# A planner's stage durations, travel times and turn shifts replaced in an attention and expert kernel

## What is computed

```python
x = x + tanh(g_xattn[0]) * L0_xattn(ctx, layernorm(x), b, lengths)      # unit 0: keys and values from the context
x = x + tanh(g_ffn[0])   * L0_ffn(layernorm(x), ...)                    # unit 1: self attention + 8 experts, top 2
x = x + tanh(g_xattn[1]) * L1_xattn(layernorm(x), ctx, ...)             # unit 2: context and own keys, then a projection
x = x + tanh(g_ffn[1])   * L1_ffn(layernorm(x), ...)                    # unit 3: causal attention, projection, layernorm, 8 experts, top 2
```

## Time and profile before

| | |
|---|---|
| time, median of 3 runs | 2508.11 us (2504.15 to 2510.68) |
| profiled execution, span from first to last instruction | 2498.3 us |
| what lies around the span, against the median | 9.8 us |
| PE, DVE, ACT, POOL busy share of the span | 86%, 64%, 56%, 53% |
| mean granted TensorE clock | 0.954 of 2.4 GHz |

### The profile page before, as it was taken

How to read it: one execution, slowest core, us unless ns; L and a number is a source line. 1 busy time by engine, 2 the same in 40 slices (tenths; PEclk the granted TensorE clock), 3 DMA queues, 4 the chain that set the end, 5 groups by cost and what they waited for, 6 DMA issues and landing times. The chain is left out here.

```text
span 2498.3 us, 53077 instructions
## 1 busy us (share of the span) xinstructions
PE 2158.4 (86%) x17514; PEld 1546.5 (62%) x17515; DVE 1595.7 (64%) x4064; ACT 1396.8 (56%) x2463; POOL 1315.6 (53%) x2193
## 2 busy tenths in 40 slices
PE   1898887899999999998899999999854999999990
PEld 1454454555556655565556666766633999999990
DVE  4787776843544787777767777777656444444445
ACT  3688885455556877766767777776631222222222
POOL 5555414467665553323323327888744565666553
PEclk9999999899999999999999999999976999999995
DMA  6878737335566775555556446665436422222224
GB/s 181 213 191 201 180 75 176 84 102 146 135 164 165 190 178 123 129 127 121 130 117 139 118 94 136 143 148 136 115 110 211 103 36 38 36 36 38 34 37 141
DMA packets 227041, 311.02 MB, mean 124 GB/s; under 512 B 30142, under 2 KB 163224, under 8 KB 220570
## 3 DMA queue, kind: packets, MB, share of 16 engines
q1 hardware_dynamic: 197450, 259.17, 41.8%
q0 software_dynamic: 22864, 36.66, 7.4%
q10 hardware_dynamic: 6528, 12.58, 1.4%
HBM read 206.67 MB, written 102.56 MB: 124 GB/s over the span
## 5 line engine op out<-in xcount | busy, mean ns | idle before, releaser
L1191 ACT ACTIVATE ex<-t_ps 128x512 f32<-128x512 f32 (+1 forms) x1280 | 684.3, 578 | 197.6 <-PE t_ps L1097 151.8
L1507 DVE TENSOR_REDUCE mx<-s_ps 128x2 f32<-128x512 f32 (+1 forms) x1024 | 658.7, 683 | 191.1 <-PE s_ps L1068 114.6
L1097 PE MATMUL t_ps<-qs,ks 123*128 123x256 bf16 x2048 | 363.2, 281 | 23.6 <-ACT ex L1191 12.6
L1120 PE MATMUL pv_ps<-ex,va 128*17 128x256 f32 (+1 forms) x5120 | 323.4, 380 | 0.9 <-POOL ex L1261 0.5
L1906 PEld LDWEIGHTS x_up_ps<-x_rows_t,x_wnow 128*128 128x128 f32 x2272 | 266.5, 193 | 5.3 <-issue 0.9
L1185 ACT ACTIVATE qs<-tr_ps 27x2048 bf16<-27x2048 bf16 x128 | 239.4, 1870 | 53.2 <-PE tr_ps L1081 49.9
L1906 PE MATMUL x_up_ps<-x_rows_t,x_wnow 128*128 128x128 f32 x2272 | 267.1, 276 | 1.1 <-DVE x_pre L1969 0.7
L1097 PEld LDWEIGHTS t_ps<-qs,ks 123*128 123x128 bf16 x2048 | 175.4, 100 | 147.7 <-ACT ex L1191 73.4
L1916 PE MATMUL x_y_ps<-wdn,x_act 128*128 x1136 | 257.1, 379 | 1.2 <-DVE x_y L1980 1.2
L1074 PE MATMUL s_ps<-ks,qs 99*128 99x256 bf16 (+1 forms) x1024 | 190.9, 290 | 55.5 <-DVE mx L1507 42.1
L1916 PEld LDWEIGHTS x_y_ps<-wdn,x_act 128*128 128x128 f32 x1136 | 210.3, 190 | 27.2 <-issue 1.6
(11 more groups left out here) (326 smaller groups left out, 4052.8 us busy)
## 6 DMA issues: line engine op xcount, KB each, us to landing
q_parts<-pq SPq DMA_DIRECT2D x128, 192.0 KB
qs<-q_parts SPq DMA_DIRECT2D x64, 384.0 KB, 5.0
qs<-q_parts SPq DMA_DIRECT2D x192, 128.0 KB, 5.9
k_parts<-pk SPq DMA_DIRECT2D x96, 192.0 KB
ks<-k_parts SPq DMA_DIRECT2D x96, 192.0 KB
ks<-k_parts SPq DMA_DIRECT2D x288, 64.0 KB
ks<-ctx_k_parts SPq DMA_DIRECT2D x64, 192.0 KB
ks<-ctx_k_parts SPq DMA_DIRECT2D x192, 64.0 KB
```

Source lines behind the costliest of these rows:

```text
L1097: last = pe.matmul(dst[:, t * T:(t + 1) * T], key[0:ROWS, h, t * P:(t + 1) * P], qs[q_at][0:ROWS, h, :], start=True, stop=True)
L1120: last = pe.matmul(pv_ps[i * VS:i * VS + VW, q0:T], val[:, t, k * QH + i, :], e, start=r == 0 and t == 0, stop=r == srcs - 1 and t == NT - ...
L1191: act.activation(ex[:, n % EXPS, 0:w], t_ps[n % 2][:, 0:w], ACT.Exp).then_inc(t_read, 1)
L1507: dve.tensor_reduce(dst, s_ps[n % S_BANKS][:, :].rearrange("p (a b) -> p a b", a=dst.shape[-1]), AX.X, ALU.max).then_inc(s_read, 1)
```

## The change

The stage table is rewritten. Each stage now has two figures, how long it holds its engine and how long until its result is there. Three lines of it, and what replaces `HOPS` and the single `NEAR_US`:

```diff
-    "MOE": [("dve", 1.95)],
-    "T": [("pe", 0.222), ("act", 0.6)],
-HOPS = {"pe": 0.2, "dve": 0.1, "act": 0.1, "pool": 0.15, "sp": 0.0, "wire": 0.1}
-NEAR_US = 0.05
+    "MOE": [("dve", 1.65, 1.8)],
+    "T": [("pe", 0.235, 0.42), ("act", 0.482, 0.614)],
+ARRIVE = {"pe": 0.145, "dve": 0.024, "act": 0.024, "pool": 0.07, "sp": 0.05, "wire": 0.0}
+ENGINES = ("wire", "sp", "pe", "dve", "act", "pool")
+NEAR_US = {"wire": 0.02, "sp": 0.3, "pe": 0.02, "dve": 0.1, "act": 0.06, "pool": 0.15}
```

A table shifts a step's turn, in jobs, for each unit (and for some steps each half or quarter). Two of its 48 lines, and where it acts:

```diff
+LATER = {
+    "OT": ((-33.7, -7.6), (-23.2, -7.8), (-16, -16.2), (-17.5, -25.7)),
+    "MOE": ((0,), (0,), (-5.3,), (0,)),
...
+def arrive(source, engine):
+    return 0.0 if source == engine else ARRIVE[engine]
+def part_of(step):
+    name, k = step[0], step[3]
+    return k[0] // HG if name in ("S", "T") else k if name in ("M", "MT", "ROWSK", "ROWSC") else k // (HG // QH) if name in ("PV", "OT") else 0
+def later(step):
+    return LATER[step[0]][step[1]][part_of(step)] if step[0] in LATER else 0.0
+def scored(u, b):
+    return [("T", u, b, (h, src)) for h in range(H) for src in range(sources(u))]
...
-            pick = min((x for x in found if x[0] <= soon + NEAR_US), key=lambda x: (x[1], rank(x[2]), x[0]))
+            pick = min((x for x in found if x[0] <= soon + NEAR_US[engine]), key=lambda x: (x[1] + later(x[2][0]), rank(x[2]), x[0]))
...
-        us = stages_of(s)[n][1]
-        begun[op], done[op] = now, now + us
+        _, held, took = stages_of(s)[n]
+        begun[op], done[op] = now, now + took
         if engine != "wire":
-            free[engine] = now + us
+            free[engine] = now + held
...
-            est[x] = max(est.get(x, 0.0), now + us + (0.0 if stages_of(x[0])[x[1]][0] == engine else HOPS[engine]))
+            est[x] = max(est.get(x, 0.0), now + took + arrive(engine, stages_of(x[0])[x[1]][0]))
```

Four waits are stated so that they hold in any order:

```diff
+                        if nth_x and JOBS[j - NX][0] == 0:
+                            sp.wait_ge(h_normed, HNX_AT[("HNX", *JOBS[j - NX], 0)] + 1)
...
-                            v, c = JOBS[j - NQ]
-                            sp.wait_ge(t_ready, T_AT[("T", v, c, (H - 1, sources(v) - 1))] + 1)
+                            sp.wait_ge(t_ready, max(T_AT[t] for t in scored(*JOBS[j - NQ])) + 1)
...
+                        if j >= 2:
+                            pool.wait_ge(tr_ready, TR_AT[("MT", *JOBS[j - 2], k)] + 1)
...
-                        if k == 0 and nth_o and JOBS[j - NO][0] == 3:
+                        if step == OT_FIRST[(u, b)] and nth_o and JOBS[j - NO][0] == 3:
```

More of the change, by code:

```diff
@@ new lines @@
+    "ROWSK": [("sp", 1.7, 1.7), ("wire", 5.5, 5.5)],
+    "ROWSQ": [("sp", 1.7, 1.7), ("wire", 6, 6)],
+    "ROWSC": [("sp", 1.7, 1.7), ("wire", 5.5, 5.5)],
+    "BPROJ": [("pool", 1.25, 1.29)],
+    "XB": [("pool", 1.25, 1.29)],
+    "STOREB": [("sp", 0.5, 0.5), ("wire", 7, 7)],
+    "HNS": [("dve", 0.95, 1.04)],
+    "HNP": [("pool", 1.05, 1.12)],
+    "HNX": [("dve", 0.64, 0.75)],
+    "HNG": [("pool", 2.57, 2.62)],
+    "HT": [("pe", 0.43, 0.61), ("act", 0.48, 0.61)],
+    "HG": [("pe", 0.85, 1.06), ("dve", 0.1, 0.18)],
@@ new lines @@
+    "PROJ": [("pe", 0.864, 1.03), ("pe", 0.864, 1.03), ("dve", 0.667, 0.76)],
+    "FIN": [("dve", 0.67, 0.76)],
+    "STOREX": [("sp", 0.5, 0.5), ("wire", 7.5, 7.5)],
+}
+STAGES_OF_UNIT = {
[8 rows of a table added]
+}
+ARRIVE = {"pe": 0.145, "dve": 0.024, "act": 0.024, "pool": 0.07, "sp": 0.05, "wire": 0.0}
+ENGINES = ("wire", "sp", "pe", "dve", "act", "pool")
+NEAR_US = {"wire": 0.02, "sp": 0.3, "pe": 0.02, "dve": 0.1, "act": 0.06, "pool": 0.15}
+LATER = {
+    "LOADX": ((-10,), (-3.2,), (-8.2,), (3.8,)),
+    "LOADC": ((14.2,), (0,), (-2.4,), (0,)),
+    "VC": ((-14.4,), (0,), (-2.3,), (0,)),
+    "LNS": ((-7.4,), (0,), (18.2,), (11.6,)),
+    "LNP": ((-47.8,), (0,), (-8.3,), (11.9,)),
+    "LNX": ((3.4,), (0,), (8.4,), (1.3,)),
+    "XT": ((38.8,), (14.3,), (20.1,), (25.4,)),
+    "KT": ((11.1,), (0,), (0,), (0,)),
+    "KSPLIT": ((6.1,), (12.4,), (20,), (-22.8,)),
+    "STACKK": ((-6.3,), (-17.4,), (-7.7,), (7,)),
+    "QSPLIT": ((10.3,), (11.6,), (11.2,), (0.2,)),
+    "STACKQ": ((-25,), (-35.8,), (-19.9,), (-46.5,)),
+    "ROWSK": ((-11.3, -21.9), (9.6, -7.5), (4.5, 19.5), (-40.5, -29.9)),
+    "ROWSQ": ((-5.8,), (-0.4,), (12.6,), (-5.1,)),
[6 rows of a table added]
+    "FIN": ((20.2,), (25.9,), (0,), (0,)),
+    "HNS": ((-8,), (0,), (0,), (-34.5,)),
+    "HNP": ((-23.3,), (0,), (0,), (-16.5,)),
+    "HNX": ((-37.4,), (0,), (0,), (-35.7,)),
+    "STOREN": ((-12,), (0,), (0,), (0,)),
+    "HT": ((6.4,), (0,), (0,), (27.2,)),
+    "HG": ((1.8,), (0,), (0,), (12.8,)),
+    "STOREX": ((21.2,), (13.3,), (-2.1,), (-26.5,)),
+    "LOADN": ((0,), (-25.8,), (0,), (0,)),
+    "K": ((0,), (-27.4,), (20.1,), (7.2,)),
+    "Q": ((0,), (0.8,), (10.9,), (6.3,)),
+    "V": ((0,), (-5.8,), (9.4,), (17.3,)),
+    "LOADY": ((0,), (0,), (-4.2,), (0,)),
+    "MOE": ((0,), (0,), (-5.3,), (0,)),
+    "ROWSC": ((0, 0), (0, 0), (-13.8, -13), (0, 0)),
+    "BPROJ": ((0,), (0,), (6.4,), (0,)),
+    "OTT": ((0,), (0,), (-47.1,), (-11.5,)),
+    "PROJ": ((0,), (0,), (5,), (7.4,)),
+    "XB": ((0,), (0,), (13,), (0,)),
+    "STOREB": ((0,), (0,), (4.8,), (0,)),
+    "HNG": ((0,), (0,), (0,), (-34.5,)),
+    "RC": ((0,), (1.8,), (0,), (0,)),
+    "RX": ((0,), (29.3,), (0,), (0,)),
+    "RANK": ((0,), (-8.7,), (0,), (0,)),
+    "RH": ((0,), (1.8,), (0,), (0,)),
+    "TH": ((0,), (-9.9,), (0,), (0,)),
+    "NAME": ((0,), (-15.1,), (0,), (0,)),
+    "XR": ((0,), (-29.2,), (0,), (0,)),
+    "XTT": ((0,), (-2.2,), (0,), (0,)),
+    "XE": ((0,), (-16.6,), (0,), (0,)),
+    "XS": ((0,), (34,), (0,), (0,)),
+}
@@ L121, in stages_of @@
     return STAGES_OF_UNIT.get((step[0], step[1]), STAGES.get(step[0]))
+def arrive(source, engine):
[5 more added lines that the diff above has]
+    return LATER[step[0]][step[1]][part_of(step)] if step[0] in LATER else 0.0
 def turns(step):
[L126 removed]
+    return sum(stage[0] == "pe" for stage in stages_of(step))
 def heads_of(g):
@@ L307, in can_begin @@
                     return None
-                at = done[reader] + HOPS[stages_of(reader[0])[reader[1]][0]]
+                at = done[reader] + arrive(stages_of(reader[0])[reader[1]][0], stages_of(s)[n][0])
             if name == "T" and len(had) >= EXPS:
@@ L337, in orders @@
             first += 1
-        for engine, mine in ready.items():
+        for engine in ENGINES:
             found = []
+            mine = ready.get(engine, [])
             for op in mine:
@@ L398 @@
 PV_AT = counted(of_kind("pe", "PV"))
+OT_FIRST = {s[1:3]: s for s in reversed(of_kind("dve", "OT"))}
 TR_AT = counted(of_kind("pe", "MT", "OT"))
```

58 lines of the change are left out of this document (33 added, 25 removed), and 18 rows, old and new, of tables (LATER, STAGES, STAGES_OF_UNIT).

## The result

The changed kernel took 2381.38 us (median of four, 2380.03 to 2386.21) beside 2506.13 us for the kernel before (2502.93 to 2510.68): a ratio of 0.9518, 95% interval 0.9499 to 0.9537. The profiled execution has a span of 2379.3 us against 2498.3, so 119 us are to be found in it.

What follows compares the result with a forecast made beforehand. PE's work was taken to bound attention, with idle PE and low clock to win; +2 - 12 - 20 - 22 - 6 = -58 us on a span of 2498.3, plus 9.8 added back, gave 2450 us, range 2430 to 2470.

Steps and rivals of the forecast that it cites:

- The four waits: Restated waits in the order: they name steps done long before, so they were costed at nothing.
- rival 3: Gains are half: splits still meet MOE in unit 2, the stretched choosing gives back what it fills; 2482 us, chance 0.12.
- The start: Start of the kernel: all seven token loads go ahead of the first context, +2 us, bounds 0 and +6.
- Unit 2, -22 for the pattern: Unit 2, images 9 to 15: shorter MOE and shorter PE waits save 3.1 us an image, bounds 0 and -31.
- Rest of unit 2, 0: Unit 2 outside the pattern: PE's own work, so 0; bounds +8 and -10, shared with the expert tiles.
- The choosing, -20: Choosing of experts: 72 reductions inside it instead of 30 give PE work, net -20 us, bounds 0 and -27.
- the tiles, 0: Expert tiles: PE's own work, so 0; bounds +8 and -10, shared with the rest of unit 2.
- Unit 0, -12: Unit 0: half of 18.5 us of waits and a third of the low clock won, bounds 0 and -30.
- unit 3, -6: Unit 3: half of 11.0 us of PE waits won, -6 us, bounds +3 and -12.
- Span and median: Whole kernel: 9.8 us between span and median added back to the forecast span of 2440.3 us.
- Rival 2: Order better everywhere, unit 2 beyond its fast part, unit 0 near its bound: 2392 us at the extreme, 2415 middle; chance 0.14.
- Rival 5: Nothing to measure: filled time is lost at the next place, PE's idle time being overstated; 2508 us, chance 0.07.

Runs made afterwards that it cites:

- waits_only: The kernel before, its own orders, with only the four restated waits of the change: ratio 0.9996 to the kernel before.
- before_no_adds: The kernel before with three of the four instructions adding the expert rows left out for images 9 to 15 of unit 2: ratio 0.9890.
- after_no_adds: The changed kernel with three of the four instructions adding the expert rows left out for images 9 to 15 of unit 2: ratio 0.9510.
- choosing_glued: The changed kernel with RC 9 to 13 and RC 14 to 19 of the choosing each in one piece again on DVE: 2386.28 us, ratio 0.9534.
- tile_shifts_only: The changed kernel with the turn shifts of the ten steps RC to XS alone, 0 for all steps of attention: ratio 1.0001.
- before_clear: The kernel before with the expert-row adds and layernorm statistics of images 9 to 15 four reductions earlier on DVE in unit 2: 2516.1 us, ratio 1.0049.
- [2532]: Mark of runs on chips where the kernel before, run beside, took 2530 to 2534 us.
- [2505]: Mark of runs on chips where the kernel before, run beside, took 2502 and 2504 us; the result itself is of this kind.
- before_apart: The kernel before with the layernorm statistics of images 9 to 15 of unit 2 moved two reductions behind their MOE on DVE: ratio 0.9947.

## Why the prediction was wrong

**What held.** The bound (PE, idle time and low clock), the place of every gain, the 656 us left alone, and the direction of nearly every sign named: no PE wait over 2 us in unit 2, the once-an-image line every 33.8 us (35 to 36 forecast), clock 1.00, the wait of 14.9 us gone, the first copy later. Only the last copy came earlier, not later, and unit 2 began 50 us earlier, not 30. The four waits cost nothing that shows (`waits_only`). The slowing of rival 3 is there: the adds take 1.79 us alone and 3.94 beside a split, which agrees with the lock that "SBUF — State Buffer" of the Trainium skill describes, as cited ahead. In the new order it met `MOE` in only two of the seven images, for 0.5 us each.

**The start**, +2: measured +3 by the cuts (107 instead of 104).

**Unit 2, -22 for the pattern.** Right in kind and nearly in size. By `before_no_adds` three of the four adds cost 26 us, by `after_no_adds` 2 remain, so 24 to 25 were won. The walk kept 1.3 us of waits an image and 2.5 us for `MOE`; measured are 0.3 (1.9 us in the window, six images) and 1.78.

**Rest of unit 2, 0: the step that failed.** Some 22 of the unit's 47 us came from it, as the two kernels without the adds also show (569 and 547 us); the bound that I had set was -10. The working held that what is left is "PE's own work", from one window, 1300 to 1438, at 97%. Two mistakes lie in it. First, these windows left out 205 of the unit's 595 us. They read, in the kernel before:

```profile
463.00:555.00 92.00, 84.28 (x635) 54.66 (x632) 56.09 (x122) 48.91 (x92) 58.99 (x80) 0.96 0.37 103
...
920.00:1048.00 128.00, 119.72 (x1074) 76.34 (x1072) 101.13 (x193) 93.78 (x159) 43.08 (x77) 1.00 0.54 134
1438.00:1515.00 77.00, 74.02 (x678) 49.59 (x676) 55.37 (x198) 60.94 (x104) 28.05 (x56) 1.00 0.44 101
```

The first row is of unit 1. In the other two, 8.3 + 3.0 = 11 us of idle PE stood unpriced. Second, 97% is not a bound: 34.3 us an image became 33.3 (133 us for four), at 99.4%. In the sum over the unit PE's idle time went from 41.5 to 9.6 us and its busy time from 553.5 to 538.4, which is 47. The fall in busy time is the clock's: 27 us of the unit were at half clock before, none after. To put idle PE that no large named wait accounts for at nothing failed in units 0, 1 and 3 too, but nowhere by as much.

**The choosing, -20, and the tiles, 0.** Unit 1 gave 34. The stretch of the choosing bears the forecast out: 398:463 had 19.7 us idle and a clock of 0.79, worth 13.7 us more; 382:438 has 7.3 idle and 0.94, worth 3.4. That is 23 us, an estimate, since the two stretches do not hold the same work. The other 11 or so are in the three stretches behind it, where I had put 0, the first of them never read (clock 0.96, the first row above). The delay was sized about right: counted from the end of unit 0 (398 us before, 383 after), the first tile was copied 23 us later, against 27 forecast. But the 71 copies then spanned 251 us instead of 266, a gain that I had put at 0, so by the clock of the whole run the first came only 7 us later and the last 7 us earlier. My mechanism, that taking the long piece apart brings the gain, is not shown. Both runs on the choosing's own places (`choosing_glued`, `tile_shifts_only`) found some 4 us. That they pay only beside attention's steps placed so that PE has work would fit these runs; no run shows it. That the net came near the 20 of the forecast is thus no proof of the mechanism.

**Unit 0, -12, and unit 3, -6.** Measured -19 and -21. I halved the waits that the view of waits names (18.5 and 11.0 us). They went to 11.9 and 5.6, by a third and by half. But idle PE was 40.4 and 26.7 us by the windows, and went to 25.4 and 12.9; smaller entries of the same view went with it. In unit 0 PE's wait for the exponentials fell from 5.5 to 1.9 us, and one of 3.9 us for the `MT` copies is no longer listed. The low clock of unit 0, of which I had counted a third as won, stayed (0.97 in both windows).

**Span and median.** I added 9.8 us for launch and end. The changed kernel's profiled execution took 2381.02 us with a span of 2379.3, so launch and end are 1.7 us, and the kernel before has the same later (2501.15 us and 2499.4). The other 8 us were the profiled execution's being shorter than the median of the three. As -58 is a difference, the forecast hardly suffers: against the later median of 2506.13 it would be 2448 instead of 2450.

In one line: over 104 to 1842 PE was idle for 162 us, and over 107 to 1724 after the change for 81; the time at half clock went from 102 to 38 us, worth 32 more. The sum started from the 71 us of waits on maxima at the top of the view and from the low clock next to them. Rival 2 ("better everywhere than I dare count") was the case, and even its extreme of 2392 lies above what was measured; 0.14 was too little for it, since the idle time to pay for it stood in the rows. Rival 5's reason points the wrong way: if PE's busy time holds waits, its idle time is understated, not overstated.

What stays open: how the gain divides among single shifts, in units 0 and 3 altogether, and which of them removed the 22 us in the rest of unit 2. The parts of the table that were run don't add up, and the border shifts hide in each other's units.

## What to carry to other kernels

Where a change rewrites the order of a whole schedule, price it from the idle time of the bounding engine over all of its span, clock included, and leave no stretch without a window. That is a ceiling (here 162 us of idle time and 51 lost to the clock, of which 81 and 32 were won); named waits give a lower estimate. A stall is a property of two lists: before moving a long piece on the waited-for engine, look at what the waiting engine's own list holds beside it, since even shortening the piece can lengthen the wait (`before_clear`). And judge a part of such a table by the end of all units, not by its own unit, and on more than one chip if one can.

## What the runs showed of the hardware

One program took 250.8 us from the first to the last tile copy in one execution and 303.4 in another, at the same data and list. The two groups of runs never share a chip in the record, and on each chip all executions of a kernel agree within 0.7%. So the chip, or something that goes with it, is likely what differs; no run shows it apart from the rest. The same line and window in the changed kernel's two profiles, [2532] first and the result's second:

```profile
L1542 DVE COPY work<-pre_ps x71: 415/425/426, 520.6 to 824.0; 128x256 f32<-128x256 f32 x71
490.00:830.00 340.00, 289.41 (x1874) 185.32 (x1867) 149.93 (x307) 158.06 (x308) 203.49 (x271) 0.92 0.48 124
...
490.00:830.00 340.00, 320.66 (x2344) 213.28 (x2347) 192.12 (x405) 204.15 (x394) 234.26 (x323) 0.99 0.61 157
```

The kernel before lost 28 us of unit 1 there (551 us in `waits_only`, 523 in its own profile), the changed one 55; that this is because its unit 1 is packed more tightly was not tested. From the issue of a tile's gather to its transpose, by the 71 pairs of rows of each, passed 21.8 us in the median instead of 16.1, and GpSimd's issue of it was hardly longer (984 and 981 ns in the mean). The packets of the queue that carries these transfers took no longer either, by the view of DMA in 500:830, [2532] first (packets, MB, share of the 16 engines' time):

```profile
q0 software_dynamic: 6816, 17.71, 18.8%
...
q0 software_dynamic: 6816, 17.71, 18.5%
```

So the time is lost around the packets, not in them. No [2532] profile has a landing for these transfers, while each [2505] profile has some, so where the time goes, ahead of the packets or behind them, stays open.

The clock fell with short waits also where PE was otherwise full. In unit 2 of the kernel before, six of seven waits of 2.23 us had half clock for 3.4 or 6.8 us during or right behind them. In `before_clear` all seven waits of 3.62 us had it for 6.8 us, in `before_apart` three of seven waits of 1.12 us for 3.4 us, and the changed kernel in 1010:1247, with waits of at most 0.4 us, shows 1.00.
